# A two-layer transformer block on one core: side steps moved between slots of TensorE's order, two turns shortened, and two turnings moved from TensorE to VectorE and DMA

## What is computed

```python
x = x + 0.5 * _L0_ffn_ref(_layernorm(x), W, b, V_r, C)      # one matmul once W + C V_r' is folded
x = x + _L0_attn_ref(_layernorm(x), ...)
x = x + 0.5 * _L0_ffn_ref(_layernorm(x), W, b, V_r, C)
x = x + 0.5 * _L1_ffn_ref(_layernorm(x), ...)               # 8 experts, top 2, and a shared one
x = x + _L1_attn_ref(_layernorm(x), ...)
x = x + 0.5 * _L1_ffn_ref(_layernorm(x), ...)

# L0 attention: 16 heads of width 8; q, k of unit length; two steps
state = q
for _ in range(2):
    sim = jnp.einsum('bqhd,bkhd->bqhk', state, k)
    att = jax.nn.softmax(sim, axis=-1)
    state = jnp.einsum('bqhk,bkhd->bqhd', att, v)
# L1 attention: a mask of 64-token blocks, the heads a plain reshape of (512, 128), one softmax step
```

## Time and profile before

| | |
|---|---|
| Time, median of 3 runs | 3888.49 us (3873.29 to 3897.85) |
| The profiled execution, its own time | 3882.77 us |
| Its span, first to last instruction | 3881.0 us |
| TensorE busy | 3390.9 us, 87% |
| VectorE busy | 2382.1 us, 61% |
| ScalarE busy | 2157.3 us, 56% |
| GpSimd busy | 1063.2 us, 27% |
| Mean granted TensorE clock | 0.927 |

### The profile page before, as it was taken

How to read it: one execution, slowest core, us unless ns; L and a number is a source line. 1 busy time by engine, 2 the same in 40 slices (tenths; PEclk the granted TensorE clock), 3 DMA queues, 4 the chain that set the end, 5 groups by cost and what they waited for, 6 DMA issues and landing times. The chain is left out here.

```text
span 3881.0 us, 55455 instructions
## 1 busy us (share of the span) xinstructions
PE 3390.9 (87%) x20374; PEld 1726.9 (44%) x20374; DVE 2382.1 (61%) x5217; ACT 2157.3 (56%) x2817; POOL 1063.2 (27%) x2225
## 2 busy tenths in 40 slices
PE   4888888898998989898998989899898989988887
PEld 2334343344444434444453444444344444444454
DVE  2335565666756666675766667576766757566573
ACT  1444566565565655556566655566665555664432
POOL 3122213141422314141231414133231413212231
PEclk7789799898999989999998989899998989998898
DMA  1000000000000000000000000000000000010110
GB/s 37 1 1 28 4 28 4 28 29 31 27 28 29 4 31 28 31 29 31 25 7 28 29 31 29 31 26 7 28 28 31 29 31 26 7 50 4 53 31 31
DMA packets 71259, 95.85 MB, mean 25 GB/s; under 512 B 40304, under 2 KB 58160, under 8 KB 70864
## 3 DMA queue, kind: packets, MB, share of 16 engines
q1 hardware_dynamic: 70992, 92.29, 7.4%
HBM read 82.76 MB, written 4.78 MB: 23 GB/s over the span
## 5 line engine op out<-in xcount | busy, mean ns | idle before, releaser
L734 ACT ACTIVATE probs<-ps 128x1024 f32<-128x1024 f32 x1536 | 1574.6, 1025 | 979.8 <-PE ps L598 944.4
L897 DVE TENSOR_REDUCE negmax<-ps 128x2 f32<-128x1024 f32 x1024 | 1251.9, 1223 | 740.0 <-PE ps L639 731.2
L598 PE MATMUL ps<-qT,kT 32*128 32x512 f32 x3072 | 811.5, 524 | 326.7 <-ACT probs L734 307.8
L615 PE MATMUL ps<-probs,v 128*32 128x512 f32 x6144 | 885.7, 651 | 0.0
L598 PEld LDWEIGHTS ps<-qT,kT 32*128 32x128 f32 x3072 | 300.4, 192 | 1008.2 <-ACT probs L734 644.4
L1105 POOL TENSOR_TENSOR xe<-xT_m,G 128x512 f32<-128x512 f32 x288 | 368.6, 1283 | 1103.1 <-PE ps L676 879.8
L676 PE MATMUL ps<-xe,w_sb 128*128 128x256 f32 x2304 | 648.8, 407 | 19.9 <-POOL xe L1105 14.4
L639 PE MATMUL ps<-kT,qT 32*128 32x512 f32 x2048 | 549.0, 531 | 66.4 <-DVE negmax L897 66.4
L676 PEld LDWEIGHTS ps<-xe,w_sb 128*128 128x128 f32 x2304 | 405.0, 195 | 252.3 <-issue 174.4
L764 ACT ACTIVATE th<-ps 128x256 f32<-128x256 f32 x576 | 221.9, 385 | 337.1 <-PE ps L676 334.1
L962 DVE SCALAR_TENSOR_TENSOR th<-th,ps 128x256 f32<-128x256 f32 x576 | 238.7, 414 | 225.2 <-ACT th L764 212.8
(11 more groups left out here) (170 smaller groups left out, 2900.6 us busy)
## 6 DMA issues: line engine op xcount, KB each, us to landing
G<-gates_dram SPq DMA_DIRECT2D x96, 768.0 KB, 6.2
v<-v_tok SPq DMA_DIRECT2D x256, 18.0 KB, 1.9
X<-in_x SPq DMA_DIRECT2D x16, 256.0 KB, 8.1
out<-X SPq DMA_DIRECT2D x16, 256.0 KB, 2.3
w_sb<-in_w SPq DMA_DIRECT2D x1, 1152.0 KB, 5.5
w_sb<-in_w SPq DMA_DIRECT2D x1, 576.0 KB, 6.4
gates_dram<-gT SPq DMA_DIRECT2D x32, 18.0 KB
wqkv<-in_wqkv SPq DMA_DIRECT2D x2, 192.0 KB, 2.5
```

What stands on the lines that cost most here:

```text
L598: nc.tensor.matmul(ps[:, B_ST + h, :], kT[a][rows, g * S + kc * P:g * S + (kc + 1) * P], qT[a][rows, g * S:(g + 1) * S], start=True, stop= ...
L615: ins = nc.tensor.matmul(ps[ROWS * j:ROWS * (j + 1), B_UT, :], v[:, at:at + ROWS], probs[:, n % QUADS, j, :], start=(kc == 0), stop=(kc == ...
L734: nc.scalar.activation(probs[:, quad % QUADS, j:j + 2, :], ps[:, B_ST:B_ST + 2, :], ACT.Exp).then_inc(sem["exp_done"], 1)
L897: nc.vector.tensor_reduce(negmax[job_no(kind, b, g) % 2][:, tc, 2 * half:2 * half + 2], ps[:, B_SM:B_SM + 2, :], AX_X, ALU.max, negate=Tru ...
```

## The change

**The side steps' places.** `close()` now keeps a load per slot in units of a slot, from a table of costs. An `m_gu` or `m_down` goes only into a slot whose load stays at or below 1.0, the other side steps into one that stays at or below 1.3; else the step tries the next slot. `behind` ties steps to the ones that they need. As `st` and `pv` together count 0.70 and `m_gu` 0.47, the two no longer share a slot. The distance between two `m_gu` becomes two slots.

**The two first turns** are 72 and 80 slots instead of 96, with windows and jobs in places of their own. All `warm` matmuls go (`WARM` is empty).

**The state** of an S1 window stays off TensorE. VectorE turns the PSUM bank in blocks of 32x32 (each head's 32 rows against 32 tokens), divides, writes high part twice and low part, and turns back; POOL copies that to `qT`. ScalarE copies `uts` for S2 and L1 alone. The turned layout puts a token in another column than before.

**The maxima.** They are gathered in columns 0 to 15 of a 32-column tile and turned by VectorE in 32x32 blocks (`negmaxT`). Four small DMAs on SP then put them in rows 24, 56, 88 and 120 of `maxrow`, and POOL adds `maxrow` to `qT`. `mx_fill`, TensorE's `rows` and VectorE's add go. The masks' constants for L1 are changed so that one row carries the maximum.

```diff
-UNIT = 1.75
+PV_AT = 3.3
...
+FFN0_AT, P0_AT, P0_OP_AT = -37, -28.5, (-11, -9, -5, 2)
+O0_AT, MOE0_AT, UNIT0, P1_AT = 5, 30, 1.75, 69
+O1_AT, MOE1_AT, UNIT1 = 85, 80, 1.75
+
+EARLY = 2
+TURNS = [72, 80] + [TURN] * NB
+STARTS = [sum(TURNS[:i]) for i in range(NB + 4)]
+EARLY_S1_AT, EARLY_S2_AT, EARLY_MAX_AT = (0, 8, 16, 24), (32, 42, 52, 62), (16, 26, 36, 46)
+EARLY_MOE0_AT, EARLY_UNIT, EARLY_P1_AT = 27, 1.1, 58
...
+WARM = ()
+
+COST = {**{n: 0.25 for n in "ffn_xt p0_xt p1_xt o_t m_xt p0_op p1_op turn m_gt m_logits".split()},
+        "ffn_y": 0.48, "o_y": 0.48, "p0_qkv": 0.36, "p1_qkv": 0.36, "m_gu": 0.47, "m_down": 0.28, "warm": 0.22,
+        "st": 0.22, "sm": 0.0, "pv": 0.48}
+FULL, OVER = 1.0, 1.3
+FILLERS = ("m_gu", "m_down")
...
 LAG = {
-    "act": {n: HOP for n in "st ffn_xt p0_xt p1_xt o_t m_xt p0_op p1_op state m_gt m_gu".split()},
-    "dve": {**{n: HOP for n in "sm ffn_y p0_qkv p1_qkv turn rows o_y m_logits m_down m_probs".split()},
-            "m_gu": 2 * HOP},
-    "pool": {**{n: HOP for n in "ffn_stats p0_stats p1_stats m_stats p0_sums p0_hi p1_hi m_index".split()},
-             "turn": 2 * HOP},
+    "act": {**{n: HOP for n in "st ffn_xt p0_xt p1_xt o_t m_xt p0_op p1_op m_gt m_gu".split()}, "p1_op": 1.0},
+    "dve": {**{n: HOP for n in "sm ffn_y p0_qkv p1_qkv turn o_y m_logits m_down m_probs".split()},
+            "m_gu": 1.8, "turn": 1.4, "p1_qkv": 1.0},
+    "pool": {**{n: HOP for n in "ffn_stats p0_stats p1_stats m_stats p0_sums p0_hi p1_hi m_index state".split()},
+             "rows": 2 * HOP},
     "sp": {"m_gt": 2 * HOP, "p1_values": HOP},
...
+            if key in self.behind:
+                other, gap = self.behind[key]
+                ready = placed[other] + gap if other in placed else pos + 0.5
+                if pos < ready:
+                    put_back((ready, i, name, args))
+                    continue
...
+                slot = int(pos // 1)
+                now = load.get(slot, 0)
+                if now + COST[name] > (FULL if name in FILLERS else OVER):
+                    put_back((slot + 1.05, i, name, args))
+                    continue
...
+                load[slot] = now + COST[name]
+                if load[slot] > FULL:
+                    load[slot + 1] = load.get(slot + 1, 0) + load[slot] - FULL
...
-        if b == 0 and kind != "L1" or b == 1 and kind == "S1" or b == NB - 1 and kind == "L1":
-            t.at(start + i + 0.5, "warm", kind, b, g, i)
     for kc in range(TC):
-        t.at(start + 2 * kc + 3.3, "pv", kind, b, g, kc)
+        t.at(start + 2 * kc + PV_AT, "pv", kind, b, g, kc)
     t.at(start + 10.2, "uts", kind, b, g)
-    t.at(start + 11.2, "turn", kind, b, g)
     if kind == "S1":
-        t.at(start + 14.2, "state", b, g)
+        t.at(start + 11.2, "state", b, g)
+    else:
+        t.at(start + 11.2, "turn", kind, b, g)
...
+            def rows(n, kind, b, g):
+
+                target = maxrow[ADD0::ROWS, :].rearrange("j (t b q) -> j b t q", t=TC, b=NG)
+                sp.wait_ge(sem["mx_ready"], n + 1)
+                if n:
+                    sp.wait_ge(sem["rows_added"], n)
+                for i in range(NG):
+                    sp.dma_start(target[:, i],
+                                 negmaxT[ROWS * i:ROWS * i + NG * TC, :]).then_inc(sem["rows_in"], 16)
...
-                    pe.wait_ge(*read(("state", b, g)))
+                    pe.wait_ge(sem["state_done"], no[("state", b, g)] + 1)
...
-            def rows(n, kind, b, g):
-                pe.wait_ge(sem["mx_ready"], n + 1)
-                turn_chunks(("rows", kind, b, g), [mx[:, NG * tc:NG * (tc + 1), :] for tc in range(TC)])
...
+                if kind == "S1":
+                    return
+                act.wait_ge(sem["state_done"], states_up_to(n))
...
+            def uts_state(n, kind, b, g):
+
+                if kind != "S1":
+                    return
+                if no[("state", b, g)]:
+                    dve.wait_ge(sem["state_done"], no[("state", b, g)])
+                dve.wait_ge(sem["pv_done"], TC * (n + 1))
+                nc.vector.transpose(uts[:],
+                                    ps[:, B_UT, :]).then_inc(sem["ut_copied"], 1)
+                dve.wait_ge(sem["ut_copied"], n + 1)
+                link(nc.vector.reciprocal(rden[:], s1t[:, :, HD]))
+                link(nc.vector.tensor_tensor(st8[:], s1t[:, :, 0:HD],
+                                             rden[:].unsqueeze(2).to_broadcast([P, TC * NG, HD]), ALU.mult))
+
+            def state(n, b, g):
+
+                twice = qstack[:, :, 0:2 * HD].rearrange("p x (r d) -> p x r d", r=2).bitcast(F32R)
+                link(nc.vector.tensor_copy(twice, st8[:].unsqueeze(2).to_broadcast([P, TC * NG, 2, HD])))
+                link(nc.vector.tensor_tensor(qstack[:, :, 2 * HD:3 * HD].bitcast(F32R), st8[:], qstack[:, :, 0:HD],
+                                             ALU.subtract))
+                nc.vector.transpose(uts[:],
+                                    qstack[:].rearrange("p x e -> p (x e)")).then_inc(sem["state_turned"], 1)
...
-            def mx_fill(n, kind, b, g):
+            def mx_turn(n, kind, b, g):
                 dve.wait_ge(sem["sm_read"], 2 * TC * (n + 1))
-                nc.vector.tensor_copy(mx[:, :, ADD0:ROWS],
-                                      negmax[n % 2][:].rearrange("p c j -> p (c j)").unsqueeze(2)
-                                      .to_broadcast([P, TC * NG, ROWS - ADD0])).then_inc(sem["mx_ready"], 1)
-
-            def rows(n, kind, b, g):
-                key = ("rows", kind, b, g)
-                target = qT[layer(kind)][:, g * S:(g + 1) * S]
-                dve.wait_ge(*filled(key))
-                nc.vector.tensor_tensor(target, side_bank(key), target.bitcast(F32), ALU.add).then_inc(read_signal(key), 1)
-                dve.wait_ge(*read(key))
-                dve.sem_inc(sem["rows_added"], 1)
+                if n:
+                    dve.wait_ge(sem["rows_in"], 16 * NG * n)
+                nc.vector.transpose(negmaxT[:], negmax[n % 2][:]).then_inc(sem["mx_ready"], 1)
...
-            def turn(n, kind, b, g):
-                if kind == "S1":
-                    m = no[("state", b, g)]
-                    pool.wait_ge(sem["state_hi"], m + 1)
-                    nc.gpsimd.tensor_tensor(qstack[:, :, 2 * HD:3 * HD].bitcast(F32R), st8[:], qstack[:, :, 0:HD],
-                                            ALU.subtract)
-                    nc.gpsimd.tensor_copy(qstack[:, :, HD:2 * HD], qstack[:, :, 0:HD]).then_inc(sem["state_lo"], 1)
+            def state(n, b, g):
+                pool.wait_ge(sem["state_turned"], n + 1)
+                nc.gpsimd.tensor_copy(qT[0][:, g * S:(g + 1) * S],
+                                      uts[:]).then_inc(sem["state_done"], 1)
+
+            def rows(n, kind, b, g):
+                target = qT[layer(kind)][:, g * S:(g + 1) * S]
+                pool.wait_ge(sem["rows_in"], 16 * NG * (n + 1))
+                nc.gpsimd.tensor_tensor(target, maxrow[:], target.bitcast(F32), ALU.add).then_inc(sem["rows_added"], 1)
```

182 lines of the change are left out of this document (93 added, 89 removed).

## The result

The changed kernel takes **3684.0 us** (median of 4, 3676.5 to 3690.0) against 3890.7 on the same chip, a ratio of 0.9474 with a 95% interval of 0.9436 to 0.9512: 5.3% less. 3610 was forecast, with a range of 3500 to 3730.

What follows compares the result with a forecast made beforehand. TensorE bounds: a slot costs the 1.64 us floor or TensorE's longer work. Savings of 196 (steady turns) + 30 (turns 0, 1) + 28 (turns 2, 3) + 20 (rest) = 274 us off 3888.5 give 3614, stated as 3610; range 3500 to 3730.

Steps and rivals of the forecast that it cites:

- The slot rule and the counts: Steady turns: each slot costs the 1.64 us floor or TensorE's longer work; new slot counts sum to 203.4 us, not 218.1.
- I take the half-clock share as gone: Steady turns: the 6.1 us a turn from slots at half clock was taken to vanish.
- 3 us for all waits: Steady turns: 0.3 us per VectorE chain and 0.2 per second `m_gu` pair, +3 us a turn; bounds 0 and 10.
- The argument on the light stretch: Slots 16 to 32, at half clock with almost no side work, would fill; only one slot a turn stays without any.
- VectorE's chain: State turning on VectorE, four times a turn: 0.68 us per transpose, 2.6 us a chain, 10.4 a turn.
- I charge nothing: POOL's contention with VectorE was put at zero; at most 1.27 us for each of four chains, 5 us.
- Waiting there holds up only `m_xe`: POOL's added work, +11 us a turn, would delay only `m_xe`, which has some two slots of slack: no cost.
- The maxima's way: DMAs on SP plus POOL's add take 5.9 us, mostly hidden; one S2 window stalls 0 to 5 us, nothing extra charged.
- The first turns: Shortening turns 0 and 1 saves 29 + 26 us, less 25 for half clock without warm-ups: 30 us.
- Clock: Rival: TensorE at half clock as often as before, 6 us in each of 14 turns: about 3710; 0.25 shared with VectorE.
- VectorE couples: Rival: maxima banks return late in every pair, 217 to 221 us a turn: 3750 to 3800, half 3680; 0.25 with Clock.
- Late rows: Rival: the maxima's DMAs come late at every window, eight stalls a turn, up to 4170 us; chance 0.04.

Runs made afterwards that it cites:

- w1: Changed kernel plus 17 filler matmuls a turn, result unread, in and before the waiting slots of turns 2 to 15: 3658.9 us.
- c2: Changed kernel with the edits of b1 and g3, w2's fillers and eight fillers a turn in turns 2 to 15: 3566.6 us.
- t1: Changed kernel with the placing, position table and 96-slot turns of before, so only state and maxima are turned by VectorE: 3894.4 us.
- b1: Changed kernel with GpSimd's bias add to the second projection's X moved 1.6 slots later, behind the copy of the turned state: 3662.4 us.
- g3: Changed kernel with the row DMAs 1.1 slots earlier in SyncE's order, ahead of the gates' broadcast for one job: 3639.8 us.
- s1: Changed kernel with the first two turns back at the full 96 slots, windows placed as in other turns: 3723.7 us.
- w2: Changed kernel plus filler matmuls, result unread, in every second slot of turns 0 and 1 and eight more: 3651.0 us.
- t2: t1 plus eleven filler matmuls a turn, result unread, in or near the half-clock slots of turns 2 to 15: 3810.9 us.
- g1: Changed kernel with the second expert layer's head, including the gates' broadcast, four slots earlier on all engines: 3717.0 us.

## Why the prediction was right or wrong

The measured 3684 us lies in the stated range, 74 us above the forecast and above its band of 3550 to 3670. In a steady turn the work at full clock came out 6.1 us shorter than the sum, and half clock and waits cost 13.6 us more than the 3 that were charged. That the first hid nearly half of the second is luck.

- **The slot rule and the counts: right.** The slots hold what the prediction counted, and no steady `pv` shares with `m_gu`. At full clock they are 1.64, 1.78, 2.21 and 2.86 us without `pv` and 1.83, 2.35 and 2.55 with it: 197.3 us a turn instead of 203.4. `pv` alone came out 0.18 shorter than the 2.01 of the sum.
- **"I take the half-clock share as gone", and 3 us for all waits: the step that failed.** Half clock was 24.8 us a turn against 23.0 before. Half clock and waits add 16.6 us to the 197.3, where 0 and 3 were charged. The argument on the light stretch held: 20.9 of the 23.0 us had been in slots 17 to 31, and 2.5 are left there, nearly all in slot 22. But half clock now stands at and behind waits, at slots 11, 12, 22, 37 to 39 and 76 to 84, with 24.5 us. There TensorE waits for a maximum (2.0, 1.3 and 1.1 us in the mean at slots 11, 22 and 37) or, at slot 80, for the projection (2.7). w1, which fills there, takes half clock to 6.5 us but the turn only by 2.9. So half clock is not the whole of the 16.6: in w1 and in c2 (6.2 us of it) the turn is still 13.8 and 8.9 us above 197.3, with at most 6.4 and 3.0 for the fillers. Most of what is left must be waits; no run takes them out alone.
- **VectorE's chain: right in length, short in what it costs.** The transposes take 0.71 us (0.68 forecast), a chain 2.78 in the mean (2.6). But TensorE's waits for the maxima in turns 4 to 14 rose from 28.8 to 82.7 us, 4.9 a turn where 3 was charged, and nothing was charged for the half clock behind them. (The page's 45.9 us more over the whole span is less than that, since these waits fell in turns 0 to 3, from 25.7 to 13.9.) With the same chains in the old placing (t1) they are 36.6 us, 0.7 a turn more than before, so it is chain and packing together that cost.
- **"I charge nothing" for GpSimd beside VectorE: wrong by 1 to 2.4 us a turn.** One chain of four meets the bias add: up to 1.08 us of standing, and the wait and half clock behind it (b1). The Trainium skill (SBUF — State Buffer, Who interferes with whom) says that a VectorE instruction with two SBUF inputs contends with a GpSimd one that reads SBUF, that the second to issue is blocked until the first is done, and that `tensor_reduce` never contends on this chip. The trace agrees on both: 15 of 15 multiplies beside the add are long, while 552 of the 1024 maxima, read from PSUM, run beside GpSimd and none takes over 1.23 us. The long cast that the prediction called fitting has one SBUF input, so that sentence does not speak of it.
- **"Waiting there holds up only `m_xe`", charged with nothing: wrong by 3 to 5 us a turn** (4.7 measured, against 1.4 between turns of the same order). The window at slot 80 was indeed not late. What waited was GpSimd's queue, with the projection's normalization in it (g3).
- **The maxima's way: right.** In slot 11's job it takes 4.9 us from `mx` to the add's end (5.9 forecast), with four DMAs issued in 2.2 us (at most 2.7). Behind the v DMAs of turn 8 the add ends at 1871.7 and its window opens at 1875.4. In the whole run the scores' matmuls waited for the add 5 times, 3.8 us together.
- **The first turns: right in the total, 325 us together for 335, but not in its terms.** The shortening alone is worth 34 us (s1) where 55 was put. Half clock in turn 0 rose from 68.3 to 129.7 us, and the fillers of w2 won back 28.6 us, for 25 taken. Yet with full turns and no `warm` matmuls (s1) the two took 359.3 us against 364.7 before. So something else in them made up for the clock, and no run takes that apart.
- **Turns 2 and 3: 15.7 us less, not 28.** Their half-clock time rose from 85.1 to 129.7 us. *Turn 15 and the rest:* 26.9 less, not 20.
- **The sum:** 112 + 39 + 16 + 27 = 194 us of the profiled span, against 274. The steady turns are 84 us short of it, the others together 4 us ahead.
- **Of the rivals,** Clock came closest in mechanism (half clock as before), though not in place. VectorE couples only in the chains, not in every `pv` slot; "more than 5 us a turn beyond before" was its sign, and 4.9 were seen. Late rows and a slower kernel did not come. "The clock of turn 8 at 0.95 or less" was named as the sign of being wrong, and it was seen: 0.93.

## What to carry to other kernels

Work taken from TensorE can come back as half clock (t1): look at what the granted clock will do in the stretch that is relieved, and try a few filler matmuls where slots are light or where the engine has just waited. For an in-order queue ask not only when a waiting instruction's result is due, but what is queued behind it and who waits for that; here one entry in a DMA order was worth some 40 us. Keep VectorE's operations on two SBUF operands away from GpSimd's long ones.

## What the hardware showed that I had not expected

With 16 groups of transposes less, the kernel took 225.3 us a turn instead of 224.2 (t1), and with eleven matmuls more it took 218.5 (t2). Half clock held through 130 of turn 0's 158 us although TensorE had matmuls in every slot and never stood still for more than 1.21 us; one matmul more in every second slot and eight besides took that to 41 us. A VectorE multiply of 0.29 us stood still for up to 1.08 us beside one GpSimd add: it ended 0.15 us after the add in all 15 cases. In g1 three multiplies that had started 0.14 to 0.15 us before GpSimd's product took 0.29 us beside it.
